# Motif terms of a fused attention and motif block on one core: the accumulating store of the odd slab goes out two shifts behind that of the even slab

## The chip, the cores and the metric

The kernel runs on one core of a Trainium2 chip. The metric is the device time of one launch in microseconds (us): the median of 3 runs was 1446.81 us before the change (1444.57 to 1449.93). The profiled execution of the same kernel took 1437.17 us, of which its span, from the first to the last instruction, is 1435.4 us.

## The reference, cut to what matters

Input x is (2, 128, 128, 96), float32. Two blocks are added to it, each behind a group normalisation. The first is a channel attention with 1x1 and 3x3 depthwise convolutions. The second, with 16 groups of 8 rows (the rows y are its channels), is where the change lies:

```python
x = x + _L0_conv_ref(_gn(x), ...)          # attention
x = x + _L1_conv_ref(_gn(x))               # motif block
# in _L1_conv_ref, for each image, f = _gn(x):
slices = [feature[:, :, ki:ki + Hm, kj:kj + Wm] for ki in range(K) for kj in range(K)]
motif = patches.reshape(B, G, Cg * 9, L).reshape(B, G, 9, Cg, L)
...                                        # nearest channel u_max and count c_max per group and tap
motif_nn = jnp.take_along_axis(motif, u_max[..., None, None], axis=3)
term = jnp.floor(motif * motif_nn * c_max[..., None, None] / Cg)
out_ser = motif * batch_mask + term
...
out = out.at[:, :, :, ki:ki + Hm, kj:kj + Wm].add(ser2[:, :, :, k])     # for each of the 9 taps
```

So each of the nine taps (shifts) gives a floor of a scaled product of two planes, and these are summed at the tap's place.

## The kernel before, in words

`build` (line 1789) runs, for image b = 0 and then 1, `attention`, `motif_grams` (the distances, and which neighbour each plane has) and `motif_terms` (line 1543). The change lies in motif_terms alone. Each call of it is a block in which the five queues run side by side and meet on semaphores.

The 128 planes of the image stand on the 128 partitions. Each is cut into N = 8 slabs of R = 16 rows of 96 values. `steps` goes over the slabs in pairs, and within a pair over the nine shifts, with the even and the odd slab in turn: (2m, shift 0), (2m+1, shift 0), (2m, shift 1), and so on. A step is one slab with one shift, 72 per image. In each step

- VectorE (DVE, `product`, L1603) multiplies a slab of f (`fc`) by the neighbour's values in `near`, giving `prod`; two steps later `overshoot` (L1716) compares prod with its rounded value and gives `over`;
- ScalarE (ACT) rounds prod in two passes (L1752, L1757) to `rnd`;
- TensorE (PE) adds rnd (L1780) and subtracts over (L1784) into one of two accumulators `acc`, one for each slab of the pair;
- the SP queue copies 16 partitions of `near2` over those of `near` for the next shift (L1632; called a move below). It is issued when the product two steps before it is done, and the product of its own step waits for it (`moved`).

Beside that, POOL's queue (GpSimd, software descriptors) gathers the neighbours of the slabs of the next pair (L1660, `gather`, called at L1683) at shifts 1 and 3 (near) and 5 and 7 (near2), each behind the product of its step, and SP loads the next pair's rows of f (L1638, by the helper of L1621) at shift 5. When a pair is through, ACT copies the two accumulators into `done_rows` (L1742, at shift 0 of the next pair), and POOL adds them to the output in memory with an accumulating store of 768 KB for each slab (L1668, `add_out`, called at L1684). The copy of the slab after next into the same done_rows waits for that store (`stored`, L1741). The last two slabs are added by DVE (L1732) and stored by SP. In the trace of the first image near and done_rows lie in the room of the next image's `img`, so they go by that name there.

The order on POOL is the order of its loop. Before the change both calls stand at shift 2:

```python
if sh in (1, 3, 5, 7) and i + 2 < N:
    product_made(pool, n)
    ...
    gather(i + 2, sh // 4, part_run(i + 2, h), h)
if i >= 2 and sh == 2:
    add_out(i - 2)
```

Of the kernel before, what the change touches and what calls it, by code (L numbers as in the profile page):

```python
# [1524 lines left out]
def motif_terms(nc, b, k, x, room, shared, fc_ahead, f_dram, out, gram_sems, att_sems):  # L1525
# [11 lines left out]
    with ExitStack() as ctx:  # L1537
# [40 lines left out]
        def product_made(eng, n):  # L1578

            eng.wait_ge(prod_p if on_pool[n] else prod_v, sum(p == on_pool[n] for p in on_pool[:n + 1]))  # L1580

        def product_inputs(eng, n):

            i, sh = steps[n]
            s = i % SLOTS
            if sh == 0:
                eng.wait_ge(near_in[s], landings(i))
                if i < 2:
                    eng.wait_ge(fc_ahead, 32 * (b + 1))
                else:  # L1590
                    eng.wait_ge(fc_in[s], 16 * ((i - 2) // SLOTS + 1))
                eng.wait_ge(edged, 2 if i == N - 1 else 1)
            else:
                eng.wait_ge(moved[i % 2], 16 * (8 * (i // 2) + sh))
            if n >= PRODS:
                eng.wait_ge(over_done, n - PRODS + 1)  # L1596

        def product(vec, n):
            i, sh = steps[n]
            s, (dy, dx) = i % SLOTS, TAPS[sh]  # L1600
            fv = fc[:, s, :].rearrange("p (r c) -> p r c", c=C)[:, :, dx:dx + WM]
            nv = near[:, s, :].rearrange("p (r c) -> p r c", c=C)[:, 2 - dy:2 - dy + R, 0:WM]
            return vec.tensor_tensor(prod[:, n % PRODS], fv, nv, ALU.mult)  # L1603

        def run(i):

            a = (first_row(i) - (R * i - 2)) * C
            return slice(a, a + (last_row(i) - first_row(i)) * C + WM)

        def part_run(i, h):  # L1610

            a, mid = run(i).start, run(i).start + HALF * C
            return slice(a, mid) if h == 0 else slice(mid, run(i).stop)
# [42 lines left out]
        @block.gpsimd  # L1656
        def _(pool):
            def gather(i, second, cells, h=0):
                s = i % SLOTS
                pool.indirect_dma_start(  # L1660
                    (near2 if second else near)[:, s, cells], None, f_dram.rearrange("y (e o) -> (y e) o", o=1),
                    bass.IndirectOffsetOnAxis(ap=index[:, second, h, i:i + 1], axis=0)
                ).then_inc((near2_in if second else near_in)[s], 16)

            def add_out(i):

                pool.wait_ge(out_ready, i + 1)
                pool.dma_start(out_p[:, R * i * C:(R * i + R) * C], done_rows[:, i % OUTS, :], accum_op=ALU.add  # L1668
                               ).then_inc(stored[i % OUTS], 16)

            nc.gpsimd.memset(near[:, 0, 0:2 * C], 0.0).then_inc(edged, 1)
            pool.wait_ge(indexed, 1)
            for second in range(2):
                gather(0, second, run(0))
                gather(1, second, run(1))
            pool.wait_ge(indexed, 2)
            for n, (i, sh) in enumerate(steps):
                if sh in (1, 3, 5, 7) and i + 2 < N:
                    product_made(pool, n)
                    if sh == 1 and i + 2 == N - 1:  # L1680
                        nc.gpsimd.memset(near[:, (i + 2) % SLOTS, R * C:NR * C], 0.0).then_inc(edged, 1)
                    h = sh // 2 % 2
                    gather(i + 2, sh // 4, part_run(i + 2, h), h)  # L1683
                if i >= 2 and sh == 2:  # L1684
                    add_out(i - 2)
                if on_pool[n]:
                    product_inputs(pool, n)
                    product(nc.gpsimd, n).then_inc(prod_p, 1)
# [166 lines left out]
```

## Time and profile before

| What | Value |
|---|---|
| median of 3 runs | 1446.81 us (1444.57 to 1449.93) |
| the profiled execution | 1437.17 us |
| its span | 1435.4 us |
| PE busy | 1302.0 us (91%) |
| DVE busy | 1123.1 us (78%) |
| ACT busy | 887.5 us (62%) |
| POOL busy | 635.8 us (44%) |
| motif terms, first image | about 476 to 740 us of the span |
| motif terms, second image | about 1172 us to the end |

The shares are averages over stages with different limits. A row of the trace's timeline gives start, duration, engine, line, operation and what it writes and reads; in brackets stands how long the engine was idle before it, and for whom. For a transfer, the time from issue to landing is a separate figure, since the issue itself takes well under that. A row of the stretches table gives the stretch and its length, then the busy time of PE, PEld (weight loads), DVE, ACT and POOL with the number of instructions, and last PE's granted clock as a share of full speed, the share of the DMA engines' time and GB/s.

### The profile page before, as it was taken

The page shows a single profiled execution, that of the slowest core. Times are in us where ns is not written, and L with a number is a line of the kernel's source. Part 1 is how long each engine was busy: PE and PEld are TensorE (multiplying, and loading weights), DVE is VectorE, ACT ScalarE, POOL GpSimd, SP SyncE. Part 2 cuts the span into 40 slices and gives each one's busy share as a digit, 9 for nine tenths or more (in the row PEclk, how much of TensorE's full clock was granted, in tenths as well). Part 3 has the DMA queues.
Part 4 walks back from the last instruction along what each step waited for, and adds up shares of the span by engine and source line. Part 5 has one row for each costly group of instructions (what it writes and reads, how often), then busy time and mean ns, then how long its engine had stood idle before and what let it go on. Part 6 is the DMA issues. An engine that isn't in the chain of part 4 may idle for free. (4 is left out here: it accounts for less than half of the span.)

```text
span 1435.4 us, 34146 instructions
## 1 busy us (share of the span) xinstructions
PE 1302.0 (91%) x13586; PEld 1051.4 (73%) x13586; DVE 1123.1 (78%) x1896; ACT 887.5 (62%) x1013; POOL 635.8 (44%) x672
## 2 busy tenths in 40 slices
PE   3899999986999499999979999999779959999998
PEld 1799997985999255555549999989679945555554
DVE  6587775568763799999967777737877739999998
ACT  3567663212552499999956666531145419999996
POOL 4889992442220253343039999624323114444400
PEclk9999999998999699999999999999989969999999
DMA  5466731892134345464427886239105234264433
GB/s 218 129 210 214 218 96 32 255 262 118 46 132 180 132 138 126 127 166 101 133 86 225 255 250 189 75 107 275 35 2 243 112 136 142 78 179 119 139 74 106
DMA packets 77173, 210.28 MB, mean 146 GB/s; under 512 B 15450, under 2 KB 15558, under 8 KB 74326
## 3 DMA queue, kind: packets, MB, share of 16 engines
q1 hardware_dynamic: 62510, 158.10, 35.0%
q0 software_dynamic: 6720, 36.93, 9.7%
q10 hardware_dynamic: 7784, 13.07, 3.3%
q8 instruction: 107, 1.75, 0.5%
q14 instruction: 52, 0.43, 0.1%
HBM read 91.54 MB, written 67.04 MB: 110 GB/s over the span
## 5 line engine op out<-in xcount | busy, mean ns | idle before, releaser
L1780 PE MATMUL acc<-rnd,ident 128*128 128x376 f32 x1152 | 392.8, 484 | 13.6 <-ACT rnd L1757 13.6
L1780 PEld LDWEIGHTS acc<-rnd,ident 128*128 128x128 f32 x1152 | 216.8, 192 | 134.5 <-ACT rnd L1757 15.0
L954 PE MATMUL ps_a<-wa,shared 128*128 128x192 f16 x1536 | 295.0, 246 | 2.6 <-DMA xc<-low 1.5
L954 PE MATMUL ps_a<-wb,xb 128*128 128x192 f16 x1536 | 294.0, 245 | 0.0
L1752 ACT ACTIVATE rnd_m<-prod,plus_round,scale 128x1504 f32<-128x1504 f32 x144 | 235.6, 1636 | 38.8 <-DVE prod L1603 29.5
L1716 DVE SCALAR_TENSOR_TENSOR over<-prod,scale,rnd 128x1504 bf16<-128x1504 f32 x144 | 255.0, 1773 | 0.0
L572 POOL TENSOR_TENSOR vt<-z 96x256 f32<-96x256 f32 x248 | 241.6, 995 | 3.8 <-ACT z L848 3.6
L1757 ACT ACTIVATE rnd<-rnd_m,minus_round 128x1504 f32<-128x1504 f32 x144 | 223.2, 1550 | 4.7
L1660 POOL DMA_INDIRECT near<-f_planes,index x42 | 120.4, 2867 | 148.0 <-DVE prod L1603 141.9
L954 PE MATMUL ps_a<-wfa,shared 128*128 128x96 f16 x1536 | 155.7, 206 | 5.9 <-issue 5.6
L954 PE MATMUL ps_a<-wfb,xb 128*128 128x96 f16 x1536 | 155.8, 205 | 0.9 <-issue 0.9
L954 PEld LDWEIGHTS ps_a<-wa,shared 128*128 128x128 f16 x1536 | 150.1, 98 | 4.3 <-DMA xc<-low 2.5
L954 PEld LDWEIGHTS ps_a<-wb,xb 128*128 128x128 f16 x1536 | 150.1, 98 | 0.0
L954 PEld LDWEIGHTS ps_a<-wfb,xb 128*128 128x128 f16 x1536 | 137.3, 98 | 5.6 <-issue 5.6
L954 PEld LDWEIGHTS ps_a<-wfa,shared 128*128 128x128 f16 x1536 | 139.5, 98 | 2.0 <-issue 1.9
L1603 DVE TENSOR_TENSOR prod<-shared,near 128x1504 f32<-128x1504 f32 x72 | 123.4, 1713 | 14.1 <-DMA near<-f_planes,index 7.1
L638 DVE TENSOR_TENSOR qk<-y_s,qk 128x384 f16<-128x384 f32 x128 | 99.8, 780 | 41.3 <-ACT qk L873 40.7
L1603 DVE TENSOR_TENSOR prod<-shared,img 128x1504 f32<-128x1504 f32 x72 | 123.3, 1714 | 6.9 <-DMA img<-near 6.6
L954 PE MATMUL ps_a<-wc,xc 102*128 102x192 f16 x512 | 126.8, 248 | 0.0
L1784 PE MATMUL acc<-over,minus_ident 128*128 128x376 bf16 x576 | 116.9, 326 | 7.8 <-DVE over L1716 7.6
L1784 PEld LDWEIGHTS acc<-over,minus_ident 128*128 128x128 bf16 x576 | 48.7, 98 | 99.5 <-DVE over L1716 65.6
L873 ACT ACTIVATE qk<-y_s 128x384 f16<-128x384 f32 x128 | 67.0, 523 | 83.2 <-DVE y_s L631 81.7
(344 smaller groups left out, 2463.9 us busy)
## 6 DMA issues: line engine op xcount, KB each, us to landing
xb<-shared ACTq DMA_DIRECT2D x64, 195.0 KB, 2.8
f_planes<-img SPq DMA_DIRECT2D x8, 1536.0 KB, 14.2
shared<-f_planes SPq DMA_DIRECT2D x16, 768.0 KB, 5.5
v_a<-shared SPq DMA_DIRECT2D x40, 260.0 KB, 2.6
v_b<-xb SPq DMA_DIRECT2D x40, 260.0 KB, 3.0
shared<-v_a SPq DMA_DIRECT2D x40, 260.0 KB, 4.4
xb<-v_b SPq DMA_DIRECT2D x40, 260.0 KB, 5.1
v_c<-xc SPq DMA_DIRECT2D x40, 195.0 KB, 3.5
```

The lines of the kernel that those rows point to most:

```text
L572: last = nc.gpsimd.tensor_tensor(out[:, i], row(p_), row(q_), op)
L638: nc.vector.tensor_tensor(qk[:, n % 4, :, C2:2 * C2], y[:, n % 2], qk[:, n % 4, :, 0:C2], ALU.subtract).then_inc(qk_lo, 1)
L873: nc.scalar.activation(qk[:, n % 4, :, 0:C2], y[:, n % 2], ACT.Copy).then_inc(qk_hi, 1)
L954: mm = lambda a, w, first, end: nc.tensor.matmul(out(i), a, w, start=first, stop=end)
L1603: return vec.tensor_tensor(prod[:, n % PRODS], fv, nv, ALU.mult)
L1660: pool.indirect_dma_start((near2 if second else near)[:, s, cells], None, f_dram.rearrange("y (e o) -> (y e) o", o=1), bass.IndirectOffset ...
L1716: nc.vector.scalar_tensor_tensor(over[:, n % 2], prod[:, n % PRODS], scale[:, sh:sh + 1], rnd[:, n % RNDS], ALU.mult, ALU.is_lt).then_inc( ...
L1752: nc.scalar.activation(rnd_m[:, n % 2], prod[:, n % PRODS], ACT.Identity, bias=k["plus_round"][:, 0:1], scale=scale[:, sh:sh + 1]).then_in ...
L1757: nc.scalar.activation(rnd[:, n % RNDS], rnd_m[:, n % 2], ACT.Identity, bias=k["minus_round"][:, 0:1]).then_inc(rnd_done, 1)
L1780: nc.tensor.matmul(o(m), k["ident"][:, :], rnd[:, n % RNDS, BR * m:BR * m + BR, :], start=False, stop=False, skip_group_check=True)
L1784: last = nc.tensor.matmul(o(m), k["minus_ident"][:, :], over[:, n % 2, BR * m:BR * m + BR, :], start=False, stop=(sh == KK - 1), skip_grou ...
```

## The change

One condition: an odd slab's accumulating store is issued at shift 4 instead of shift 2. Even slabs keep shift 2.

```diff
--- before.py
+++ after.py
@@ -1681,7 +1681,7 @@
                         nc.gpsimd.memset(near[:, (i + 2) % SLOTS, R * C:NR * C], 0.0).then_inc(edged, 1)
                     h = sh // 2 % 2
                     gather(i + 2, sh // 4, part_run(i + 2, h), h)
-                if i >= 2 and sh == 2:
+                if i >= 2 and sh == 2 + 2 * (i % 2):
                     add_out(i - 2)
                 if on_pool[n]:
                     product_inputs(pool, n)
```

On POOL, in the first image, pair of slabs 2 and 3 (img is near and done_rows there, and a row "x2" stands for two instructions, of the even and the odd slab; the rows ahead of the store are gathers of shift 1, those behind it of shifts 3 and 5):

```order
 L1660 DMA near<-f_planes,index 128x862 x2
 L1660 DMA img<-f_planes,index 128x864 x2
-L1668 DMA out<-img 128x1536 x2
+L1668 DMA out<-img 128x1536
 L1660 DMA img<-f_planes,index 128x862 x2
+L1668 DMA out<-img 128x1536
 L1660 DMA near<-f_planes,index 128x864 x2
 L1660 DMA near<-f_planes,index 128x862 x2
```

The second store has moved behind both gathers of shift 3. The same piece stands in the second image, and pair 4 and 5 has it as well, with the gathers of the odd slab in rows of their own:

```order
 L1681 MEMSET img 128x192
 L1660 DMA img<-f_planes,index 128x864
-L1668 DMA out<-img 128x1536 x2
+L1668 DMA out<-img 128x1536
 L1660 DMA img<-f_planes,index 128x862
 L1660 DMA img<-f_planes,index 128x670
+L1668 DMA out<-img 128x1536
 L1660 DMA near<-f_planes,index 128x864 x2
 L1660 DMA near<-f_planes,index 128x862
```

Here too the odd store goes behind the second gather of shift 3. In the last pair (6 and 7) there are no gathers, and the two stores follow each other as before. No other engine's order changes. On SP, in the first image, this is what is queued about shift 5 of the pair 2 and 3 (L1621 is a load of f, L1632 a move):

```order
L1632 DMA img<-near 16x1726 [waits prod_v0] x7
L1621 DMA shared<-f_planes 128x1536 [waits prod_v0]
L1632 DMA img<-near 16x1726 [waits prod_v0]
L1621 DMA shared<-f_planes 128x1536 [waits prod_v0]
L1632 DMA img<-near 16x1726 [waits prod_v0] x6
```

The last of the seven moves is that of (even slab, shift 5), the one between the loads that of (odd slab, shift 5); these rows are the same before and after.

## Rows read from the trace of the kernel before

**Rows 1.** The page's costliest groups, and stretch 1271 to 1306 us of the stretches table.
```profile
L1603 DVE TENSOR_TENSOR prod<-shared,near 128x1504 f32<-128x1504 f32 x72 | 123.4, 1713 | 14.1 <-DMA near<-f_planes,index 7.1
...
L1603 DVE TENSOR_TENSOR prod<-shared,img 128x1504 f32<-128x1504 f32 x72 | 123.3, 1714 | 6.9 <-DMA img<-near 6.6
...
L1784 PEld LDWEIGHTS acc<-over,minus_ident 128*128 128x128 bf16 x576 | 48.7, 98 | 99.5 <-DVE over L1716 65.6
...
1271.00:1306.00 35.00, 35.00 (x129) 19.05 (x129) 35.00 (x23) 33.56 (x23) 13.84 (x4) 1.00 0.42 125
```
**Rows 2.** Timeline of DVE, second image, pair of slabs 2 and 3.
```profile
1255.63 1.71 DVE L1603 TENSOR_TENSOR prod<-shared,near 128x1504 f32<-128x1504 f32 x1
...
1258.96 1.71 DVE L1603 TENSOR_TENSOR prod<-shared,near 128x1504 f32<-128x1504 f32 x1
...
1264.28 1.73 DVE L1603 TENSOR_TENSOR prod<-shared,near 128x1504 f32<-128x1504 f32 x1 [1.92 <-DMA near<-near]
...
1267.62 1.72 DVE L1603 TENSOR_TENSOR prod<-shared,near 128x1504 f32<-128x1504 f32 x1
```
**Rows 3.** Moves (L1632), issue to landing: 1290 to 1310 us; 1257.2 to 1262 us.
```profile
DMA to landing us min/median/max: 2.2/2.2/2.4
...
DMA to landing us min/median/max: 5.9/6.4/6.9
```
**Rows 4.** Timeline of POOL, same place; last, landing of the two stores (L1668).
```profile
1254.84 1.91 POOL L1668 DMA_DIRECT2D out<-done_rows  x2
1260.94 2.39 POOL L1660 DMA_INDIRECT near<-f_planes,index  x1 [4.20 <-DVE prod L1603]
1266.28 2.29 POOL L1660 DMA_INDIRECT near<-f_planes,index  x1 [2.95 <-DVE prod L1603]
...
DMA to landing us min/median/max: 9.6/11.2/12.8
```
**Rows 5.** DMA queues, 1258 to 1261 us: packets, MB, share of 16 engines.
```profile
q0 software_dynamic: 99, 0.59, 98.7%
```
**Rows 6.** DVE's waits: us, times, longest; 545 to 640 us, then 1318 to 1328.
```profile
DVE prod L1603 <- DMA img<-near: 3.6, 2, 2.3
...
DVE prod L1603 <- DMA near<-near: 1.7, 1, 1.7
```
**Rows 7.** Last pairs: landing of stores, of moves (673 to 679 us); DVE's waits, both images.
```profile
DMA to landing us min/median/max: 7.4/7.8/8.3
...
DMA to landing us min/median/max: 5.4/5.7/6.1
...
DVE prod L1603 <- DMA img<-near: 1.0, 2, 0.6
...
DVE prod L1603 <- DMA near<-near: 0.7, 2, 0.4
```
**Rows 8.** SP's queue, second image; landing of the loads (L1621), of the move of 1269.4.
```profile
1269.95 0.53 SPq L1621 DMA_DIRECT2D shared<-f_planes  x1
1272.70 0.49 SPq L1632 DMA_DIRECT2D near<-near  x1
...
DMA to landing us min/median/max: 6.0/6.1/6.3
...
DMA to landing us min/median/max: 3.0/3.0/3.0
```
**Rows 9.** Landing of the move issued at 576.5, 638.8, 1272.7 and 1334.4 us.
```profile
DMA to landing us min/median/max: 2.8/2.8/2.8
...
DMA to landing us min/median/max: 2.9/2.9/2.9
...
DMA to landing us min/median/max: 4.1/4.1/4.1
...
DMA to landing us min/median/max: 2.5/2.5/2.5
```

## The prediction

> **What bounds the kernel now.** The change touches only motif_terms, so I read the stretches in which it runs, not the page's averages. In the table of stretches [rows 1] VectorE (DVE) is busy for 35.00 of 35.00 us in a stretch without stores, and TensorE (PE) for 35.00 as well at a granted clock of 1.00. The costliest groups of the page tell which of the two sets the pace: the weight loads of the overshoot matmul stand idle for 99.5 us and 65.6 us of that wait for DVE's over [rows 1]; nothing of DVE's waits for PE but the two last additions. A step (one slab, one shift) takes DVE 3.33 us: the product starts at 1255.63 and the next at 1258.96 [rows 2]. So a gap in DVE's row is a gap in the time, and the reader should look for gaps only. The two product groups of the page have them, 14.1 and 6.9 us, all from transfers [rows 1]. 7.1 us of them is the first gather of an image, which the change does not touch.
>
> The timeline of DVE shows one of the other gaps [rows 2]: the product of (slab 3, shift 3) starts at 1264.28 where 1258.96 + 3.33 = 1262.29 was due, after 1.92 us of waiting for near<-near. That is SP's small transfer (a "move") which shifts the neighbour planes on by one. SP issues it when the product two steps before is done (1255.63 + 1.71 = 1257.34), and it has 1262.29 - 1257.34 = 4.95 us to land. In a quiet stretch moves land in 2.2 us; this one took 6.9 us and the next, issued at 1258.96 + 1.71 = 1260.7, took 5.9 [rows 3]. 6.9 - 4.95 is the 1.92 of the gap.
>
> What holds them up stands in POOL's timeline [rows 4]: at 1254.84 it issues the two accumulating stores side by side, and the next gather only at 1260.94. The stores land 9.6 and 12.8 us after their issue [rows 4], which is 1264.4 and about 1268.3; the two moves land at 1257.3 + 6.9 = 1264.2 and 1260.7 + 5.9 = 1266.6. A move issued in a store's shadow lands with that store, not before it; and the first move landed well ahead of the second store, though that was in its queue before the move was. From 1258 to 1261 the software queue has 98.7% of the 16 engines and the SP queue is not in the list at all [rows 5]. In 3 us it moves 99 packets there, so the 128 rows of one store hold the engines for 128 x 3 / 99 = 3.9 us.
>
> The same gap comes once in each of the four middle pairs of slabs (two per image): 1.3 and 2.3 us in the first image, 1.92 and 1.7 in the second [rows 2, 6] (the row of the first image sums two, 3.6 with a longest of 2.3), 7.2 us in all, 0.5% of the time. About 0.5%, 7.2 us, is also what a measurement of this kernel can tell from no change. By stalls removed alone, then, the change can reach that bound and not pass it.
>
> **The change, part by part.** Nothing is added or removed: six accumulating stores per image stay, with their bytes and their 0.9 to 1.3 us on POOL, which is idle for long stretches beside them. POOL's order shows what moves: the odd store of the two middle pairs goes behind both gathers of shift 3. In the last pair POOL has no gathers and no product to wait for, so that both stores still go out when ScalarE's copy is ready: cost of that part, nothing. The copy into done_rows that waits for the odd store comes a whole pair (18 steps of 3.33 us) later, so a store that starts some 13 us later is not waited for: nothing. The gathers of shift 3 no longer queue behind the odd store; the gather there lands well before the next pair needs it anyway: nothing.
>
> *The even store, alone now.* It is still issued at the same point, behind the same gather, and the move of (odd slab, shift 3) still falls into its shadow. Is the partner to blame for any of that move's delay? The move landed with the first store, while the second ran on for some 4 us [rows 3, 4]; what is ahead of it is the even store alone. So I take a relief of 0. The last pairs bound it: there each store goes out as its copy is ready, with no gathers about; they land in 7.4 and 8.3 us and the moves beside them in 5.4 and 6.1 us, and DVE still waits, 1.0 us in two gaps in the first image and 0.7 in two in the second [rows 7]. If the even store alone fell to that 5.4, four gaps of 0.45 would stand for the 7.2 us: a gain of 5.4 us. Ends of this term: -5.4 and 0; I take 0.
>
> *The odd store, in its new place.* Side by side it cost nothing of its own: its move (issued 1260.7, landed 1266.6) was wanted at 1267.6 only because the first gap had already pushed DVE back [rows 2, 3]. One gap paid for two stores. Two shifts on, the first gap is past and every move has its 4.95 us again. POOL issues the store behind the gather of (odd slab, shift 3), at 1266.28 + 2.29 = 1268.6 [rows 4]. The SP queue then has at 1269.95 the load of f rows for the slab after next (768 KB, landing in 6.0 to 6.3 us), at 1272.70 the move of (odd slab, shift 5), and behind it the second load [rows 8]. That move lands now in 2.8, 2.9, 4.1 and 2.5 us at the four places [rows 9]. With 3.9 us of store ahead of it and of its load it would land in 6.7, 6.8, 8.0 and 6.4 us, and DVE would stand for 1.75 + 1.85 + 3.05 + 1.45 = 8.1 us. That is the upper end. The lower: the store is issued 1.4 us before the load (1268.6 against 1269.95), and if all of that is time in which the engines had nothing else, only 2.5 us per place are pushed: 0.35 + 0.45 + 1.65 + 0.05 = 2.5 us. The gather of shift 3 fills most of this time (it is still being described until 1268.6), so I take 0.5 us per place off: 8.1 - 2.0 = 6.1 us. The second load and the move behind it come a place later and find DVE pushed back already: nothing, as with the second store before. Nothing elsewhere in the profile bounds a store beside these loads, and a gain is excluded for this term, since no gap stood there before.
>
> Sum: 0 + 6.1 = +6 us on the profiled execution's 1437.17. That execution is 9.6 us below the median of the runs (1446.81), as a whole and not in this stretch, so I put the same 6 us on the median: **1452.9 us**, +0.4%.
>
> One rule bears on where the push lands. The Trainium skill (DMA: Bandwidth & Descriptors, Queues, rings and completion order) says that each DMA engine goes round the queues it has work for, and drains a whole packet of one ring before it switches. By it the move that is waiting when the gather ends (issued 1269.4) would go between gather and store, and only what is queued behind it, the load and its move, would wait, once and by a full store; the sum by the rule alone is the upper end, 8.1 us.
>
> **The rivals.**
> *The earlier move is caught (slower).* The move issued at 1267.62 + 1.72 = 1269.4 lands in 3.0 us today [rows 8], and has 1.95 us to spare. The store enters its queue 0.8 us before it. If the engines go from the gather straight on to the store, this move takes 3.0 + 3.9 = 6.9 us and DVE stands 1.95 us; where the load's move is later still, that one decides (3.05 us at the third place): 3 x 1.95 + 3.05 = 8.9 us, and up to 12 if both gaps add partly. It decides from the point where that move lands after 4.95 us. For it: the move of 1257.3 was caught so by a store issued 2.5 us ahead of it. Against it: the second store too was in the queue by then (POOL was done with both at 1256.75), and that move went ahead of it, as this one would behind a gather. 1455.7 to 1459.
>
> *The stores hurt only as a pair (better).* Two stores together may be what makes engines fall behind, for the moves beside lone stores took 5.4 rather than 6.3 to 7.2 us. Then the even gap shrinks by 5.4 us over four places and the odd store costs its lower end, 2.5: -2.9 us, 1443.9. Against it: the first move landed with the first store. The Trainium skill's section "Issuing engines are not separate DMA queues" of the same page says transfers of all engines interleave; a fine interleaving would favour this case, but the move beside a lone store took 5.4 us against 2.2, so the trace shows none fine enough.
>
> *The whole promise.* No move is late any more, at either place: -7.2 us, 1439.6. For it nothing but the size of the slack; against it the gaps of the last pairs.
>
> *It does as good as nothing.* The odd store falls into a hole of the loads and is absorbed, the even gap stays: 0, 1446.8.
>
> **How the numbers follow.** Forecast (even gap unchanged, odd store 2.5 to 8.1 us) 0.55; earlier move caught 0.17; only as a pair 0.15; nothing 0.08; the whole promise 0.05. Slower by over 7.2 us: about three tenths of the forecast's case (its upper part, and the scatter of the medians, which is some 3 us) and most of the second, 0.17 + 0.14 = 0.31. Faster by over 7.2 us: half of the last case and a little scatter, 0.05. Within 0.5%: 0.64. The range leaves out the top of the caught-move case and most of the whole promise: 1443 to 1459.
>
> **What would show it.** In the changed kernel's profile: (1) the waits of the product for near<-near at shift 3 of the odd slab stay between 1.3 and 2.3 us, with the move landing in 6 to 7 us; (2) the move issued just after it, 5.9 us before, lands in under 3; (3) a new gap of 1 to 2.5 us on DVE some 13 us later, at the product of (odd slab, shift 5), in all four places, with that move landing in 6 to 7.5 us; (4) the page's product groups show some 6 us more idle time than 14.1 and 6.9; (5) the last pairs look as before. I am wrong if gap (1) is gone or below 0.6 us (the pair did it), if no gap stands after the odd store (it is absorbed), or if the gap comes at shift 5 of the even slab (the earlier move).

## The result, and the profile after

Over 22 runs of each kernel the changed kernel takes 1449.73 us (median; 1444.31 to 1460.71) and the kernel before 1445.61 us (1435.75 to 1455.17). The ratio is 1.0046, with a 95% interval of 1.0027 to 1.0064: the change costs 0.46%, some 6.7 us, with 3.9 to 9.3 us inside the interval; the plain difference of the two medians is 4.1 us. Every ratio in this document leaves out the few slow runs, those over 1.5% above the fastest of the same kernel. The profiled execution took 1456.99 us. That is 19.8 us more than the one of before, but single executions of one kernel differ by as much (the range above), and most of this difference lies outside motif_terms: from the first to the last product of each image the two stretches together grew by 5.9 us. What the change does has to be read from the gaps.

The product groups of the page stood idle for 14.1 + 6.9 = 21.0 us before [rows 1] and stand idle for 26.4 us now. The page of the changed kernel, costliest groups (line, engine, operation, count | busy, mean ns | idle before and what ended most of it):

```profile
L1603 DVE TENSOR_TENSOR prod<-shared,near 128x1504 f32<-128x1504 f32 x72 | 124.0, 1723 | 16.2 <-DMA near<-near 9.7
L1603 DVE TENSOR_TENSOR prod<-shared,img 128x1504 f32<-128x1504 f32 x72 | 123.9, 1723 | 10.2 <-DMA img<-near 10.0
...
L1784 PEld LDWEIGHTS acc<-over,minus_ident 128*128 128x128 bf16 x576 | 48.7, 98 | 105.4 <-DVE over L1716 71.5
```

The idle time of the overshoot's weight loads grew by much the same amount, from 99.5 to 105.4 us, and the part of it that waits for over from 65.6 to 71.5 us: DVE is late, and PE waits for it.

The timeline of DVE at the place of [rows 2] (second image, slabs 2 and 3; all of this execution is some 17 us later there) now has two gaps:

```profile
1276.07 1.73 DVE L1603 TENSOR_TENSOR prod<-shared,near 128x1504 f32<-128x1504 f32 x1
...
1280.97 1.72 DVE L1603 TENSOR_TENSOR prod<-shared,near 128x1504 f32<-128x1504 f32 x1 [1.48 <-DMA near<-near]
...
1284.31 1.72 DVE L1603 TENSOR_TENSOR prod<-shared,near 128x1504 f32<-128x1504 f32 x1
...
1287.64 1.72 DVE L1603 TENSOR_TENSOR prod<-shared,near 128x1504 f32<-128x1504 f32 x1
...
1292.53 1.73 DVE L1603 TENSOR_TENSOR prod<-shared,near 128x1504 f32<-128x1504 f32 x1 [1.48 <-DMA near<-near]
```

The product at 1280.97 is that of (odd slab, shift 3), where the one gap was before. Then come (even, 4), (odd, 4), and at 1292.53, late, (even, 5). The timeline of POOL there answers to [rows 4]:

```profile
1271.96 1.01 POOL L1668 DMA_DIRECT2D out<-done_rows  x1
1278.07 2.36 POOL L1660 DMA_INDIRECT near<-f_planes,index  x1 [5.11 <-DVE prod L1603]
1282.96 2.28 POOL L1660 DMA_INDIRECT near<-f_planes,index  x1 [2.52 <-DVE prod L1603]
1285.21 1.04 POOL L1668 DMA_DIRECT2D out<-done_rows  x1
```

The odd store goes out at 1285.21, right behind the gather of (odd, 3). The view of the SP queue's moves (L1632, 1285.9 to 1286.4 us) and that of the stores (L1668, 1285 to 1285.5 us) give the move which the late product waited for, and the store it ran into:

```profile
L1632 SPq DMA_DIRECT2D near<-near x1: 486/486/486, 1286.1 to 1286.1; - x1
DMA to landing us min/median/max: 6.5/6.5/6.5
```

```profile
L1668 POOL DMA_DIRECT2D out<-done_rows x1: 1040/1040/1040, 1285.2 to 1285.2; - x1
DMA to landing us min/median/max: 7.8/7.8/7.8
```

The move lands at 1286.1 + 6.5 = 1292.6 and the store at 1293.0, the same pattern as before. The caught move lands with the store, or nearly so: within 0.2 us of it at most even stores of both kernels (at two places of the kernel before up to 1.1 us behind it), and 0.5 to 2.8 us ahead of it at the odd ones of the changed kernel, which have a load of f beside them. The DMA queues from 1287.5 to 1289.5 us, the time in which that move would have been served, list one queue only (a packet that starts in the stretch is counted whole, so that the share can pass 100%):

```profile
q0 software_dynamic: 88, 0.45, 106.9%
```

The move behind it, that of (odd slab, shift 5), is late too: the four of them take 6.9, 7.0, 5.9 and 6.8 us to land. Yet only one costs anything, 0.25 us, since the gap at (even, 5) has already pushed DVE back.

The waits of DVE's product, in us, times and longest, at the four middle pairs (575 to 600, 640 to 656, 1276 to 1300 and 1336 to 1360 us):

```profile
DVE prod L1603 <- DMA img<-near: 3.3, 3, 1.6
...
DVE prod L1603 <- DMA img<-near: 2.9, 2, 2.4
...
DVE prod L1603 <- DMA near<-near: 3.0, 2, 1.5
...
DVE prod L1603 <- DMA near<-near: 2.8, 2, 2.3
```

That is 12.0 us where 7.2 us stood before. Split by step, 4.0 us are the old gaps (1.50, 0.51, 1.48, 0.54) and 8.0 us new ones at shift 5 (1.59 and 0.25, 2.41, 1.48, 2.30). The last pairs have 1.3 and 1.0 us against 1.0 and 0.7 [rows 7]; the change does not touch them.

### The profile page after: what moved, and what is told of

Read it like the earlier page. It is cut to its first block and busy times, and to the rows that moved or that the text cites. A ratio compares the mean times of both kernels' runs of the same rounds, so it can differ in the third digit from the quotient of the medians.

```text
span 1455.2 us, 34146 instructions
## 1 busy us (share of the span) xinstructions
PE 1315.7 (90%) x13586; PEld 1064.6 (73%) x13586; DVE 1123.8 (77%) x1896; ACT 887.5 (61%) x1013; POOL 629.5 (43%) x672
## 3 DMA queue, kind: packets, MB, share of 16 engines
q8 instruction: 107, 1.75, 0.5%
## 5 line engine op out<-in xcount | busy, mean ns | idle before, releaser
L1780 PE MATMUL acc<-rnd,ident 128*128 128x376 f32 x1152 | 392.6, 484 | 13.6 <-ACT rnd L1757 13.6
L1660 POOL DMA_INDIRECT near<-f_planes,index x42 | 113.7, 2706 | 159.0 <-DVE prod L1603 153.8
L954 PE MATMUL ps_a<-wfa,shared 128*128 128x96 f16 x1536 | 160.9, 208 | 4.0 <-issue 4.0
L954 PE MATMUL ps_a<-wfb,xb 128*128 128x96 f16 x1536 | 160.8, 208 | 2.8 <-issue 2.7
L954 PEld LDWEIGHTS ps_a<-wfa,shared 128*128 128x128 f16 x1536 | 142.8, 100 | 2.4 <-issue 2.4
L954 PEld LDWEIGHTS ps_a<-wfb,xb 128*128 128x128 f16 x1536 | 140.6, 99 | 5.4 <-issue 5.3
L1784 PEld LDWEIGHTS acc<-over,minus_ident 128*128 128x128 bf16 x576 | 48.7, 98 | 105.4 <-DVE over L1716 71.5
```

The lines of the kernel that those rows point to most:

```text
L954: mm = lambda a, w, first, end: nc.tensor.matmul(out(i), a, w, start=first, stop=end)
L1660: pool.indirect_dma_start((near2 if second else near)[:, s, cells], None, f_dram.rearrange("y (e o) -> (y e) o", o=1), bass.IndirectOffset ...
L1780: nc.tensor.matmul(o(m), k["ident"][:, :], rnd[:, n % RNDS, BR * m:BR * m + BR, :], start=False, stop=False, skip_group_check=True)
L1784: last = nc.tensor.matmul(o(m), k["minus_ident"][:, :], over[:, n % 2, BR * m:BR * m + BR, :], start=False, stop=(sh == KK - 1), skip_grou ...
```

## The experiments

Below, "even gaps" are those at shift 3 of the odd slab and "odd gaps" those that came behind the odd store, each summed over the four middle pairs in one profiled execution. "Groups" is the idle time of the page's two product groups together. Some 12 us of it stand in the first pairs of the two images in each profile of both kernels (11.8 to 12.1 us, some 7 of them the wait for the second image's first two gathers), and 2.0 to 2.6 us in the last pairs. Each kernel is named by what it does; diffs are against the kernel before.

**Do the gaps repeat?** Both kernels were profiled once more, unchanged.

> The kernel before, unchanged, profiled a second time, to learn how far the four gaps at shift 3 of the odd slab (1.33, 2.27, 1.92, 1.66 us, sum 7.2) vary between executions. Theory A (the gap is set by where the packets of store and move fall, the same every time): each within 0.4 us of its value, sum 6.5 to 8. Theory B (the difference to the changed kernel's 1.50, 0.51, 1.48, 0.54 is scatter): sum anywhere from 4 to 8, and the two places of pair 4 and 5 may come out near 0.5 us.

> The changed kernel, unchanged, profiled a second time. Its first profile has 4.0 us of gaps at shift 3 of the odd slab and 8.0 us at shift 5, at the even slab. Theory A: 3.5 to 4.5 us and 7 to 9 us again, at the same steps. Theory B: the first sum anywhere from 4 to 8 us. The rival 'earlier move caught' expects the second gap at the even slab's shift 5 again in all four places; my forecast's form (the load's move is the late one) expects it at the odd slab's shift 5 in at least two.

The kernel before: even gaps 1.51, 1.62, 1.75 and 1.50, sum 6.4, groups 20.9. The changed kernel: even gaps 1.37, 1.61, 2.38 and 1.59, sum 6.9; odd gaps 7.2, the large one again at the even slab's shift 5 in all four places (2.06, 1.66, 1.34, 1.07), with 0.18 to 0.66 us more at the odd slab's shift 5 in three; groups 28.2:

```profile
L1603 DVE TENSOR_TENSOR prod<-shared,near 128x1504 f32<-128x1504 f32 x72 | 123.6, 1716 | 17.4 <-DMA near<-near 10.6
L1603 DVE TENSOR_TENSOR prod<-shared,img 128x1504 f32<-128x1504 f32 x72 | 123.6, 1718 | 10.8 <-DMA img<-near 10.4
```

So the relief of the even gap in the first profile was largely scatter: a single gap varies by 1 us between executions (0.51 and 1.61 us at the same place), more than theory A allowed. The odd gaps are steady: 8.0 and 7.2 us. Nor did the kernel before keep within theory A (sum 6.5 to 8, each gap within 0.4 us): its second gap went from 2.27 to 1.62 us. The rival "earlier move caught" has the place right and my forecast has it wrong.

**Which store makes which gap?** Stores of one row instead of 16, in the middle pairs only, so that 15 rows of a slab are missing from the sum in memory. The diff stands for two kernels, which the remarks at its end name:

```diff
-            def add_out(i):
+            def add_out(i, rows=R):
...
-                pool.dma_start(out_p[:, R * i * C:(R * i + R) * C], done_rows[:, i % OUTS, :], accum_op=ALU.add
+                pool.dma_start(out_p[:, R * i * C:(R * i + rows) * C], done_rows[:, i % OUTS, 0:rows * C],
+                               accum_op=ALU.add).then_inc(stored[i % OUTS], 16)
...
-                    add_out(i - 2)
+                    add_out(i - 2, 1 if i < N - 2 else R)                  # both thin
+                    add_out(i - 2, 1 if i < N - 2 and i % 2 == 1 else R)   # odd thin
```

> The order of the kernel before, but in the middle pairs both stores write one of their 16 rows (the other 15 rows of slabs 0 to 3 are left out of the sum in memory). All theories in which the stores' hold on the DMA engines makes the gaps: no gap over 0.3 us at these places, the time 7.2 us below the kernel before (0.5%). If the gaps came from POOL's descriptor writing or from the gathers, they stay at 1 us or more.

> The order of the kernel before, with both stores at shift 2, but in the middle pairs the odd slab's store writes one of its 16 rows (48 of 768 KB; the other 15 rows of those slabs are left out of the sum in memory). Theory 'even store alone' (what holds the move is the store ahead of it, the partner adds nothing): four gaps at shift 3 of the odd slab, sum near 7 us as before, and no gap elsewhere; time as before within 0.2%. Theory 'only as a pair' (the partner's bytes lengthen the gap): sum 4.0 us as in the changed kernel, or less; 3 us faster.

Both thin: the even gaps are gone, what is left is 0.54, 0.29 and 0.29 us at shift 5, beside the loads of f; groups 15.8; ratio 0.9946 (0.9925 to 0.9967). POOL is as long at the two thin stores as at the whole ones (1.0 and 1.3 us). So the stores' hold on the DMA engines, and not POOL's own work, made the gaps, and they were worth the 0.5% that the profile had said. Odd thin: even gaps 1.67, 1.38, 0.78, 1.38, sum 5.2, groups 19.8, ratio 0.9992 (0.9966 to 1.0018). That lies between the two theories (near 7; 4.0 or less). Taking nearly all of the second store away buys 1.2 to 2.0 us of gaps and nothing that the times can show: the partner was not quite free, but close to it. What it did hold back was the next move, that of (even, 4), which lands in 3.4 to 3.6 us here instead of 5.9 to 6.4; before, that delay cost nothing, since DVE was already late.

**What does the odd store cost in its new place by itself?** The order of the changed kernel, with the even store thin:

```diff
-                if i >= 2 and sh == 2:
-                    add_out(i - 2)
+                if i >= 2 and sh == 2 + 2 * (i % 2):
+                    add_out(i - 2, 1 if i < N - 2 and i % 2 == 0 else R)
```

> The order of the changed kernel (odd store at shift 4), but in the middle pairs the even slab's store writes one of its 16 rows (the other 15 rows of slabs 0 and 2 are left out of the sum in memory). The odd store in its new place is then the only large one. If each store costs by itself: no gap over 0.3 us at shift 3, and at shift 5 of the even slab the gaps of the changed kernel (8.0 and 7.2 us in its two profiles), sum 6.5 to 8.5; the time about as the kernel before. If the new gaps need an even gap before them (DVE pushed back, so that product, move and load meet the store at this phase): sum under 5 us.

No gap at shift 3, but 17.1 us behind the odd store (two gaps at each of the four places, 1.69 and 2.73 us at the first, 2.93 and 0.81 us at the fourth), groups 32.2, ratio 1.0092 (1.0057 to 1.0127). I expected 6.5 to 8.5 us, and the other theory less; both are wrong, on the same side. At the first place the store lands 12.7 us after its issue and the moves issued from 575 to 579.5 us land in up to 9.5 us. The timelines of POOL and of DVE (first image) show what differs:

```profile
565.79 3.99 POOL L1660 DMA_INDIRECT img<-f_planes,index  x1 [5.09 <-DVE prod L1603]
570.08 2.96 POOL L1660 DMA_INDIRECT img<-f_planes,index  x1 [0.30 <-issue]
573.00 1.04 POOL L1668 DMA_DIRECT2D out<-img  x1
```

```profile
567.13 1.71 DVE L1603 TENSOR_TENSOR prod<-shared,img 128x1504 f32<-128x1504 f32 x1
...
582.23 1.73 DVE L1603 TENSOR_TENSOR prod<-shared,img 128x1504 f32<-128x1504 f32 x1 [1.69 <-DMA img<-near]
588.38 1.73 DVE L1603 TENSOR_TENSOR prod<-shared,img 128x1504 f32<-128x1504 f32 x1 [2.73 <-DMA img<-near]
```

POOL's gathers of shift 3 take 4.0 and 3.0 us here instead of 2.4 and 2.3, so the store goes out 573.00 - 568.84 = 4.2 us after the product of (odd, 3) is done; in the changed kernel it was 1285.21 - 1282.69 = 2.5 us. At 2.5 us it catches the move of (even, 5). At 4.2 us it misses that, and catches the move of (odd, 5), which stands behind the first load, and then that of (even, 6) behind the second: the two gaps at 582.23 and 588.38. The place of a store is worth nothing without its phase against the moves and loads.

**Is it the loads, or the gather ahead?** The odd store at shift 6, past the loads and behind the gathers of shift 5:

```diff
-                if i >= 2 and sh == 2:
+                if i >= 2 and sh == 2 + (4 * (i % 2) if i < N - 2 else 0):
```

> As the changed kernel, but the odd store of the middle pairs stands at shift 6, behind both gathers of shift 5 and past the loads of f. Theory 'loads' (in the new place the load of f in SP's queue makes the second gap, as my forecast had it): the second gap is small, under 0.6 us a place, and the time that of the kernel before or 1 us less. Theory 'behind a gather' (a store that POOL issues right behind a gather holds the next move that is issued, loads or not): a gap at shift 7 of the even slab in all four places, 0.9 to 2 us each, 4 to 7 us in all, and the time 3 to 6 us above the kernel before.

Even gaps 4.1; a gap at shift 7 of the odd slab in all four places (2.00, 0.74, 1.69, 0.77), sum 5.2; groups 24.5; ratio 1.0005 (0.9978 to 1.0032). The sum is that of the theory "behind a gather" (4 to 7), but the slab is not: it had named the even one, as in the changed kernel. The timelines of POOL and DVE (second image, first place) show why:

```profile
1283.43 3.02 POOL L1660 DMA_INDIRECT near<-f_planes,index  x1 [0.30 <-issue]
1286.46 1.00 POOL L1668 DMA_DIRECT2D out<-done_rows  x1
```

```profile
1280.58 1.72 DVE L1603 TENSOR_TENSOR prod<-shared,near 128x1504 f32<-128x1504 f32 x1
...
1295.67 1.73 DVE L1603 TENSOR_TENSOR prod<-shared,near 128x1504 f32<-128x1504 f32 x1 [1.69 <-DMA near<-near]
```

The gathers take 3.9 and 3.0 us here, so the store goes out 1286.46 - 1282.30 = 4.2 us after the product of (odd, 5). The move of (even, 7), issued 0.8 us ahead of the store, lands in 2.3 us; that of (odd, 7), 2.5 us behind the store, takes 6.7 and lands with it. The time came out 0.7 us above the kernel before where the theory said 3 to 6; the interval holds the 3.5 us that the groups gained, and holds no change as well. So a store right behind a gather costs a gap with no load about. Beside the loads the cost was 7 to 17 us instead of 5, though phase and loads changed together there.

**Can the phase be chosen?** Both stores apart, and each issued when a product is done, which is when a move is issued too:

```diff
-                if i >= 2 and sh == 2:
-                    add_out(i - 2)
+                if i in (3, 5) and sh in (2, 6):
+                    product_made(pool, n)
+                    add_out(i - 3 if sh == 2 else i - 2)
+                if (i, sh) in ((N - 2, 2), (N - 1, 3)):
+                    product_made(pool, n)
+                    add_out(i - 2)
```

> Both stores apart, and each issued only when a product is done, that is at the same moment as a move and not behind a gather: in the middle pairs the even store at shift 2 of the odd slab, the odd store at shift 6 of the odd slab; in the last pair at shift 2 of the even and shift 3 of the odd slab, each after waiting for that step's product. Theory 'phase': the move issued at the same moment reaches the engines before the store (first packets of a move 0.9 us after its issue, of a store 1.4), and the next, 3.33 us later, meets only the store's last microsecond, so moves land in 3 to 4.5 us of the 4.95 they have and no gap over 0.3 us stands at any of the six places: 7 to 8.5 us below the kernel before (0.5 to 0.6%). Theory 'a store costs a gap wherever it is': six gaps of 0.5 to 2 us, 8 to 14 us in all, and the time 3 to 6 us above the kernel before.

> The kernel with both stores apart and timed, once more (its first profile: 0.95 us of gaps in the middle pairs, 13.6 us in the two product groups of the page; ratio 0.9947). Under 2 us in the middle pairs and 12 to 15 us in the groups again; 0.4 to 0.6% below the kernel before. If the first profile was a lucky draw: 3 us or more in the middle pairs.

This is the fastest kernel that computes the whole result: 0.9947 (0.9924 to 0.9971) and, once more, 0.9938 (0.9915 to 0.9961). The groups stand at 13.6 and 13.7 us; of the 7.4 us gained in the first of them some 6.2 are in the middle pairs and 1.0 in the last, whose stores are timed too. None of the four middle pairs has a gap behind a store; 0.95 and 0.84 us are left at shift 5 beside the loads. One gap of each profile in a last pair (0.70, 1.27 us) is over the 0.3 that I had allowed. The page:

```profile
L1603 DVE TENSOR_TENSOR prod<-shared,near 128x1504 f32<-128x1504 f32 x72 | 123.5, 1716 | 10.2 <-DMA near<-f_planes,index 7.0
L1603 DVE TENSOR_TENSOR prod<-shared,img 128x1504 f32<-128x1504 f32 x72 | 123.5, 1716 | 3.4 <-DMA img<-near 3.1
```

The timeline of POOL shows the store with its wait, and the view of the moves from 1258.5 to 1262.5 us the two beside it:

```profile
1253.19 3.03 POOL L1660 DMA_INDIRECT near<-f_planes,index  x1 [0.30 <-issue]
1259.02 0.98 POOL L1668 DMA_DIRECT2D out<-done_rows  x1 [2.80 <-DVE prod L1603]
```

```profile
DMA to landing us min/median/max: 2.3/3.2/4.2
```

The move issued with the store passes ahead of it (2.3 us), the next lands in 4.2 of its 4.95 us. The wait of 2.80 us on POOL costs nothing, since POOL had it to spare.

The next move still lands with the store; what is new is that the store is through in time. In the changed kernel, whose even store goes out without its partner too, but right behind a gather, the store took 9.0 us to land at this place, and the caught move, issued 2.5 us behind it, 6.5 us. Here the store takes 7.0 us and the move, 3.1 us behind it, 4.2. So of the 2.3 us that this move gains only some 0.5 us is its later issue against the store's. The larger part goes with the sooner landing of the store, which here stands 2.8 us clear of the gather ahead of it. Each timed store of the middle pairs has this distance from the gather as well as its phase, and no run separates the two. Two figures speak for the distance: at the old 2.5 us behind a store that lands in 7.0 us the move would land in some 4.5 us by this pattern (an estimate), still in time; and in the last pair of the kernel before, whose stores have no gathers about, the move issued 1.8 us behind a store that landed in 7.4 us took 5.4 and cost 0.4 us.

**Without an added wait.** The even store ahead of the gather of (even, 3), the odd one ahead of that of (even, 7), behind the waits that these gathers have anyway:

```diff
+                    if i in (2, 4) and sh in (3, 7):
+                        add_out(i - 2 + sh // 4)
                     h = sh // 2 % 2
                     gather(i + 2, sh // 4, part_run(i + 2, h), h)
-                if i >= 2 and sh == 2:
+                if i >= N - 2 and sh == 2:
                     add_out(i - 2)
```

> No added wait: in the middle pairs the even store stands at shift 3 of the even slab ahead of that step's gather, the odd store at shift 7 of the even slab ahead of its gather, so both go out when the gather's own wait for the product is over. The last pair is as before. Theory 'phase': as in the kernel with waits, no gap over 0.4 us at the four places, 6 to 7 us below the kernel before. Theory 'a store costs a gap wherever it is': four pairs of gaps of 1 to 2 us, 3 to 6 us above it.

2.9 us in the middle pairs: 1.43 and 1.22 at shift 5 beside the loads (first image only), 0.25 behind a store; groups 16.6. The gaps say phase, though two of them are over the 0.4 us allowed; the time was to fall by 6 to 7 us, and the ratio, 0.9991 (0.9955 to 1.0027), doesn't show it. Its interval holds the 4.4 us that the groups gained, and no change as well.

**One store timed at a time, in the changed kernel.** The first piece is the kernel with the even store timed, the second that with the odd store timed:

```diff
-                if i >= 2 and sh == 2:
+                if i in (3, 5) and sh == 2:
+                    product_made(pool, n)
+                    add_out(i - 3)
+                if i in (3, 5) and sh == 4 or i >= N - 2 and sh == 2:
                     add_out(i - 2)
```

```diff
-                if i >= 2 and sh == 2:
+                if i in (3, 5) and sh == 4:
+                    product_made(pool, n)
+                if i >= 2 and sh == 2 + (2 * (i % 2) if i < N - 2 else 0):
                     add_out(i - 2)
```

> The changed kernel (odd store at shift 4, right behind the gather) with one thing more: in the middle pairs the even store is issued only when the product of (odd slab, shift 2) is done, together with a move. Theory 'phase': the even gaps (4.0 and 7.0 us in the two profiles of the changed kernel) go to under 0.5 us in all, the odd store's gaps stay at 7 to 9 us (or rise to 12, if POOL's gathers take 3.9 and 3.0 us without a gap before them, as beside the thin even store, and the store so meets both loads): page total of the two product groups 21 to 27 us, time 0 to 6 us above the kernel before. Theory 'a store costs a gap wherever it is': both sums stay, time 5 to 8 us above it.

> The changed kernel with one thing more: in the middle pairs the odd store, at shift 4 of the odd slab, is issued only when that step's product is done, together with a move and beside the loads of f. The even store is as in both kernels, with its gaps of 4 to 7 us. Theory 'phase': the move issued with the store passes; the next (even slab, shift 6) waits behind the second load and the store's end, 4.2 to 5.5 us against 4.95: new gaps of 0 to 0.6 us a place, under 2.5 us in all instead of 7 to 8, and a time within 3 us of the kernel before. Theory 'loads' (a store beside the loads costs its 3.9 us to a move in any case): 5 to 10 us of gaps at shifts 5 or 6, and the time 3 to 7 us above the kernel before.

Even store timed: the even gaps go (0.2 us in all), and the odd store then costs 15.5 us; groups 30.7, ratio 1.0083 (1.0049 to 1.0116). I had allowed for 12 and 27. At three of the four places it is the thin store's case once more: POOL's gathers take 4.0 and 2.9 to 3.0 us, the odd store goes out 4.2 us after the product and meets both loads. The fourth place shows the same rule from its other side. There the second gather took 1.32 us, so the store went out 1343.65 - 1341.12 = 2.5 us after the product of (odd, 3), and the main gap came at the even slab's shift 5 as in the changed kernel:

```profile
1343.65 1.03 POOL L1668 DMA_DIRECT2D out<-done_rows  x1
```

```profile
1339.40 1.72 DVE L1603 TENSOR_TENSOR prod<-shared,near 128x1504 f32<-128x1504 f32 x1
...
1351.65 1.73 DVE L1603 TENSOR_TENSOR prod<-shared,near 128x1504 f32<-128x1504 f32 x1 [1.90 <-DMA near<-near]
```

Within one execution, the store's delay behind the product thus decides which move is caught.

Odd store timed: even gaps 4.7, odd gaps 7.0 (1.76, 0.94, 2.21, 2.07), all at shift 6 of the even slab, the move behind the second load; groups 25.0, ratio 1.0047 (1.0009 to 1.0086). Here "phase" fails and "loads" is right: beside the loads of f the store costs a gap even when it is issued with a move. Timing is not enough if the place is wrong.

**Timing without separation.** Both stores side by side as before, after `product_made` at shift 2 of the odd slab:

```diff
-                if i >= 2 and sh == 2:
+                if i in (3, 5) and sh == 2:
+                    product_made(pool, n)
+                    add_out(i - 3)
+                    add_out(i - 2)
+                if i >= N - 2 and sh == 2:
                     add_out(i - 2)
```

> Timing without separation: in the middle pairs both stores go out side by side as in the kernel before, but only when the product of (odd slab, shift 2) is done, together with a move. If timing is what gains: the move issued with them passes, but the next one, 3.33 us later, has two stores (7.8 us) before or around it and lands in 5 to 8 us: one gap of 0.5 to 2.5 us a place, 3 to 8 us in all, and the time within 0.3% of the kernel before. If separation is not needed: under 1.5 us in all and 0.4 to 0.6% below the kernel before.

Five gaps of 0.72 to 1.28 us, sum 5.3; groups 20.7; ratio 0.9983 (0.9958 to 1.0009). Timing alone gains little if anything; separation alone loses 0.46% (odd store at shift 4) or changes nothing that can be told (at shift 6); together, and away from the loads, they gain 0.5%.

Over all of these the gaps and the measured times agree. With 21.0 us for the kernel before, 32.2 and 30.7 us of groups stand beside +0.92% and +0.83%, 26.4 to 28.2 beside +0.46%, 20.7 beside -0.17%, and 13.6 beside -0.53%. For each kernel the difference in the groups, divided by 1445 us, lies within the interval of its ratio.

## Why the prediction was right, and where it was not

*What bounds.* Right. A gap on DVE is a gap in the time, as far as the runs can tell: 5.4 and 7.3 us more in the groups, 4.1 us by the medians and 6.7 us by the ratio. Predicted 1452.9 from a median of 1446.81, a rise of 6.1; the median of more runs of before was 1445.61, and the change came out at 1449.73.

*The cause of the old gap, and the even store alone.* Right in kind. With both stores thin the gap goes; with the odd one thin it stays at 5.2 of 6.4 to 7.2 us. The relief that I took as 0 measured 4.0 to 6.9 us of even gaps in the changed kernel against 6.4 to 7.2, a relief of 1.3 us on the mean of two profiles each, which the scatter of single gaps cannot tell from 0.

*The odd store in its new place.* The step that failed is "the move of (odd slab, shift 5), behind the load, is the late one". The runs showed the move before it, of (even slab, shift 5), issued 0.9 us after the store at the place shown, to be the late one in all eight places of two profiles. I had argued that the engines would serve a waiting move between the gather and the store, since the first of two stores had let one pass. They did not: from 1287.5 to 1289.5 us only the software queue was served. I had also named a gap at this step as a sign that I am wrong, and as to the mechanism I was. The Trainium skill (DMA: Bandwidth & Descriptors, Queues, rings and completion order) says that an engine drains a whole packet of one ring before it switches; I had read that as one transfer, one turn. In that reading it did not hold here, and whether one turn took in gather and store together, the runs do not show.

The term's size came out all the same: 8.0 and 7.2 us against 2.5 to 8.1, with 6.1 taken. In part that is luck, for the gap that I had priced hardly exists (0.25 us, and 1.1 us in the second profile). The move that I had named did land late, in 5.9 to 7.4 us where I had priced 6.4 to 8.0. Against its 4.95 us that is 6.8 and 7.4 us over the four places of the two profiles, so alone it would have cost about what I took. But the move ahead of it was just as late (6.0 to 7.4 us), made the gap first and pushed DVE back. That one gap can pay for two late moves I had seen at the even store, and did not look for ahead of the load. The kernel with the thin even store shows how little the size by itself was worth: a store 1.7 us later in phase costs 17.1 us.

*The rivals.* "The earlier move is caught" named the mechanism: 8.9 us priced, 8.0 and 7.2 measured, but the time stayed under its 1455.7; the even gaps, lower by 1.3 us on the mean, take a part of it off. In chances I had given it 0.17 against 0.55. "Only as a pair" falls with the thin odd store, which left 5.2 us of even gaps where 1.8 were priced. "It does as good as nothing" falls with the new gaps at all four places. "The whole promise" was 0.05; its 7.2 us exist, as both the thin stores and the timed ones show, but this change does not collect them.

*The signs I had named.* Gap (1) stayed in the second profile and fell to 0.5 us at two places in the first, which I had called a refutation; one profile was too little for such a test. Sign (2) held in direction and not in size: the move issued after the caught one came down from 5.9 to 6.4 us to 2.3 to 3.5 in the first profile and 3.3 to 4.4 in the second, where I had said under 3. Sign (3) failed in its step and held in its size; its move does land in 5.9 to 7.4 us. Sign (4) held: 5.4 and 7.3 us. Sign (5) held.

## What to carry to other kernels

In these runs the small transfer that was issued next behind a large one was held until the large one had landed or nearly so. So ask of each large transfer which small ones are issued during it and how much slack each has. A delay costs only if nothing before it has already made the consumer late. Two large transfers side by side can so share one gap, and pulling them apart can make two of it. What helped here is to issue the large one at the same event as the small one, clear of the gathers and loads, and to check the distance to the next small one against the time in which the large one lands. How much of that was phase and how much the distance from the gather is open. And profile twice before a single gap is believed.

## What the runs showed of the hardware that I had not expected

POOL's issue of the same gather takes 3.9 to 4.0 us in some places and 2.3 to 2.4 in others, and which one it is changes with the kernel: 2.36 and 2.28 us at shift 3 in the changed kernel, 3.99 and 2.96 with a thin even store. The difference moved the next store on POOL by 1.7 us and doubled its cost. What sets it was not tried. And an accumulating store holds the 16 DMA engines longer than a plain load of the same 768 KB. The store's queue moved 0.59 MB in 3 us at 98.7% of the engines [rows 5]; SP's queue, with the loads of f and some of a move, moved 0.91 MB in 3 us at 91.8%, in the kernel before at 1273 to 1276 us. Per byte that is 1.7 times as long, about 3.9 us for a store against an estimated 2.4 for a load:

```profile
q1 hardware_dynamic: 177, 0.91, 91.8%
```

Open stays why single gaps at the same step vary between 0.5 and 1.6 us from one execution to the next, how much of the timed stores' gain is phase and how much their distance from the gather, and why the engines went on from gather to store past a waiting move here, where between two stores they let one through.
